# A transformer block on one Trainium2 core: a new order of the first transfers, with two large loads between and behind the stores of V

## The chip, the cores and the metric

One core of a Trainium2 chip. The metric is the device time of one launch in microseconds (us), lower is better. The kernel before has a median of 844.91 us over 3 runs (843.4 to 845.48).

## The reference

Two batch elements of 1024 positions with 128 features, all in float32:

```python
x = x + _layernorm(_L0_attn_ref(_layernorm(x), Wq, Wk, Wv, Wo, bo, rel_pos_bias))
x = x + _layernorm(_L0_ffn_ref(_layernorm(x), ...))      # one shared and 8 routed experts, top 2
# inside attention, 16 heads of 64:
q, k, v = x @ Wq, x @ Wk, x @ Wv                         # split into heads
logits = (q @ k.T + causal + pos_bias) / 64              # pos_bias: a table over 128 distances per head
out = (softmax(logits) @ v) @ Wo + bo
```

Each expert is a layer of 128 to 512 with GELU and one back to 128, weighted by a gate. The change touches only what lies ahead of the heads.

## The kernel before

The 2048 positions are 16 blocks of 128 (t = 0 to 15), in four quarters of four blocks. Products in float32 are made of three products of rounded halves: a tensor is split into a high part and the rest (`_hi`, `_lo`), and `three` (L1072) runs hi x hi, hi x lo and lo x hi.

**First stage, norm and V of all heads.** VectorE takes the quarters of x in turn (L815 to L827): statistics (L776, L779), a root on GpSimd (`root`, L418), Newton step and normalisation (L787 to L793). TensorE transposes each block (`transposes`, L1078), ScalarE and VectorE copy the result out as high and low part. Then `values_of_all(t)` (L1100) computes V of block t for all 16 heads, as two halves of 512 columns with three matmuls of 128x512 each, in four PSUM banks used in turn; so block t waits for the copies of block t - 2. ScalarE copies the first half and VectorE the second (`copy_v`, L613 and L808) into one of four SBUF buffers, `probs[t % 4]`, and SP stores the buffer, 512 KB, to DRAM (`store_v`, L311). A copy of block t waits until the store of block t - 4 has landed (`v_stored`). All four counts of stores are waited for (L351), then `load_v(0, 0)` brings back the columns of head 0 for the first batch element. GpSimd splits what is loaded (`split_v`, L451).

**Queues and hand-written order.** Every engine has a fixed program; nothing is planned at run time. All DMAs but two (the weight of V and bo, which ScalarE issues) are issued by SP, in program order, on one queue. SP's program is: the first loads, then for t = 0 to 15 the store of block t, with `place_q(0, 0)` (two DMAs, L320) behind t = 5 and `place_k(0, 0)` (L327) behind t = 7; then the waits for the stores, `load_v(0, 0)`, and `head(0)` (L333): `load_v(0, 1)`, `place_q(0, 1)`, `place_k(0, 1)`, and the same for the first batch element of the next head. `place_q` copies q between partitions once both halves are computed (`qk_lo`), `place_k` waits until q has been copied.

**Heads.** A head has 16 slots (s), one for each block of queries: scores on TensorE (`scores`, L1142; slot 8 is the first of the second batch element and waits for `k_copied`), row minimum with bias on VectorE (L848), exponential on ScalarE (L649), transposes of the probabilities (L1173), their product with V (L1191, first in slot 7), the output weight (L1205, first in slot 11). In slots 8 and 9 TensorE also computes q and k of the next head (`project_qk`), which waits for GpSimd's split of that head's weights (`split_wqk`, L423), in GpSimd's slot 5.

**Who reads what the change moves.** `wqk` is scaled by ScalarE at L627, behind two copies of transposed blocks and ahead of the first copies of V. `bias_all[:, 0]` is read by GpSimd at L521. `bias_all[:, 1:H]` is read by GpSimd in slot 0 of head 0 (L493), behind `split_v(0, 0)` in its program. `wo` is read by TensorE at L1205. `wr` and `layer_bias_T` (`small_loaded`) are read behind the last head (L567, L740, L981).

Of the kernel before, what the change touches and what calls it, by code (L numbers as in the profile page):

```python
# [11 lines left out]
def transformer_block(  # L12
# [23 lines left out]
    H = rel_steps.shape[1]  # L36
# [13 lines left out]
    NCH = NB // CH  # L50
# [48 lines left out]
    with ctx:  # L99
        def sb(name, shape, dt=f32):  # L100
            return ctx.enter_context(nc.sbuf_tensor(name, shape, dt))
# [4 lines left out]
        def sem(name):  # L106
            return ctx.enter_context(nc.semaphore(name))
# [11 lines left out]
        wo = sb("wo", [P, H, D])  # L119
        far = sb("far", [P, H])  # L120
        bias_all = sb("bias_all", [P, H, 2 * P])
# [32 lines left out]
        layer_bias_T = sb("layer_bias_T", [P, NE * HB + NE])  # L154
# [4 lines left out]
        wr = sb("wr", [P, E])  # L159
# [51 lines left out]
        wo_loaded = sem("wo_loaded")  # L211
        bo_loaded = sem("bo_loaded")
        acc_started = sem("acc_started")
        small_loaded = sem("small_loaded")
        bias_loaded = [sem(f"bias_loaded{i}") for i in range(2)]
# [75 lines left out]
        @block.sync  # L291
        def _(sp):
            def load_x(c):
                sp.dma_start(x_sb[:, CH * c:CH * (c + 1), :],
                             x_blocks[:, CH * c:CH * (c + 1), :]).then_inc(x_loaded[c], 16)

            load_x(0)
            load_x(1)
            sp.dma_start(wqk[:], Wqk).then_inc(wqk_loaded, 16)
            load_x(2)  # L300
            load_x(3)


            sp.dma_start(bias_all[:, 0:1, :], rel_steps[:, 0:1, :]).then_inc(bias_loaded[0], 16)
            sp.dma_start(bias_all[:, 1:H, :], rel_steps[:, 1:H, :]).then_inc(bias_loaded[1], 16)
            sp.dma_start(wo[:], Wo2).then_inc(wo_loaded, 16)
            sp.dma_start(wr[:], Wr).then_inc(small_loaded, 16)
            sp.dma_start(layer_bias_T[:], layer_bias).then_inc(small_loaded, 16)


            def store_v(t):  # L311
                sp.wait_ge(v_evac_act, t + 1)
                sp.wait_ge(v_evac_dve, t + 1)
                sp.dma_start(v_dram[t * P:(t + 1) * P, :], probs[t % 4][:]).then_inc(v_stored[t % 4], 16)

            def load_v(h, b):
                src = bass.AP(v_dram.tensor, h * DH + b * T * HD, [[HD, P], [P * HD, QB], [1, DH]])
                sp.dma_start(v_raw[b][:], src).then_inc(v_loaded[b], 16)

            def place_q(h, b):  # L320

                sp.wait_ge(qk_lo, h * (2 * B) + 2 * b + 2)
                for part in range(2):
                    sp.dma_start(q_hl[b][part * DH:(part + 1) * DH, :].bitcast(f32),
                                 k_hl[b][0:DH, part, :].bitcast(f32)).then_inc(q_copied[b], 16)

            def place_k(h, b):  # L327

                sp.wait_ge(q_copied[b], h * 32 + 32)
                sp.dma_start(k_hl[b][0:DH, :, :].bitcast(f32), k_hl[b][DH:P, :, :].bitcast(f32))\  # L330
                  .then_inc(k_copied[b], 16)

            def head(h, last=False):  # L333
                if not (isinstance(h, int) and h == 0):
                    sp.wait_ge(v_ready, h * B)
                load_v(h, 1)
                place_q(h, 1)
                place_k(h, 1)
                if not last:
                    sp.wait_ge(v_ready, h * B + 1)  # L340
                    load_v(h + 1, 0)
                    place_q(h + 1, 0)
                    place_k(h + 1, 0)

            for t in range(NB):
                store_v(t)
                if t == 5:
                    place_q(0, 0)
                if t == 7:
                    place_k(0, 0)  # L350
            for r in range(4):  # L351
                sp.wait_ge(v_stored[r], 16 * (NB // 4))
            load_v(0, 0)
            head(0)
            with sp.Fori(1, H - 1) as h:
                head(h)
            head(H - 1, last=True)

            def load_expert(i, wf, wp):
                sp.dma_start(wfc_raw[i], wf).then_inc(moe_w_loaded[i], 16)  # L360
                sp.dma_start(wproj_raw[i], wp).then_inc(moe_w_loaded[i], 16)


            sp.wait_ge(v_ready, (H - 1) * B + 1)
            sp.wait_ge(min_ready, (H - 1) * S + QB)
            load_expert(0, Wfc_s, Wproj_s.rearrange("(k p) n -> p k n", p=P))
            sp.wait_ge(v_ready, H * B)
            sp.wait_ge(min_ready, H * S)
            load_expert(1, Wfc[0, :, :], Wproj[0, :, :].rearrange("(k p) n -> p k n", p=P))

            def expert_src(e):

                return (bass.AP(Wfc.tensor, (e - 1) * (D * HID), [[HID, P], [1, HID]]),
                        bass.AP(Wproj.tensor, (e - 1) * (D * HID), [[D, P], [P * D, HB], [1, D]]))

            def reload(e, i):
                sp.wait_ge(wproj_ready, e - 1)
                load_expert(i, *expert_src(e))

            def load_gates(e, i):  # L380
                if not (isinstance(e, int) and e <= 2):
                    sp.wait_ge(gated_ready, (e - 1) * NCH)
                sp.dma_start(gate_rows[i], bass.AP(gate_dram.tensor, (e - 1) * (B * T), [[0, P], [1, B * T]]))\
                  .then_inc(gates_loaded[i], 16)

            reload(2, 0)
            sp.wait_ge(gate_T_ready, 1)
            for j in range(CH):
                sp.dma_start(bass.AP(gate_dram.tensor, j * P, [[B * T, E], [W, NCH], [1, P]]),
                             gate_T[j * E:(j + 1) * E, :, :]).then_inc(gates_stored, 16)  # L390
            sp.wait_ge(gates_stored, 16 * CH)
            load_gates(1, 1)
            load_gates(2, 0)
            with sp.Fori(3, NE - 1, 2) as e:
                for i in range(2):
                    reload(e + i, 1 - i)
                    load_gates(e + i, 1 - i)

            for c in range(NCH):
                sp.wait_ge(result_ready, c + 1)  # L400
                sp.dma_start(out_blocks[:, CH * c:CH * (c + 1), :],
                             normed[:, CH * c:CH * (c + 1), :]).then_inc(result_stored, 16)
            sp.wait_ge(result_stored, 16 * NCH)
# [667 lines left out]
        def _(pe):  # L1071
# [56 lines left out]
            def wait_shared(h, s, last):  # L1128

                uses = [u for u in SHARED_USE if u[0] < s and not (isinstance(h, int) and h == 0 and u[2] < 0)  # L1130
                        and not (last and u[2] > 0)]
                if isinstance(h, int) and h == 0 and not uses:
                    pe.wait_ge(qk_lo, NC)
                    return
                _, kind, n, b, part = uses[-1] if uses else SHARED_USE[-1]
                n = h + n if uses else h - 1
                if kind == "qk":
                    pe.wait_ge(qk_lo, n * (2 * B) + 2 * b + part + 1)
                else:
                    pe.wait_ge(wo_scaled, n * (B * NC) + b * NC + part + 1)  # L1140
# [249 lines left out]
```

## Time and profile before

| what | value |
|---|---|
| median of 3 runs | 844.91 us |
| the profiled execution | 844.46 us |
| its span | 842.7 us |
| TensorE matmuls (PE) | 771.5 us busy, 92% |
| VectorE (DVE) | 707.7 us, 84% |
| ScalarE (ACT) | 612.8 us, 73% |
| GpSimd (POOL) | 298.9 us, 35% |
| DMA | 70.72 MB, mean 84 GB/s |

Times in rows are in us from the start of the span unless marked ns. PE is TensorE's matmuls, PEld its weight loads, SPq and ACTq the issue of a DMA by SP or ScalarE. L12 is line 12 of the kernel. "x4" is the number of instructions merged into a row; in brackets stands how long the engine had been idle and what it waited for. The chain of waits is followed back from the last instruction: at each step to what released it. "issue" in it is time in which the engine waited for nothing that the profile shows. The granted clock is TensorE's, 1.00 for 2.4 GHz and 0.50 for 1.2 GHz.

### The profile page before, as it was taken

What the parts mean: (1) busy time and instruction counts of PE and PEld (TensorE: products, weight loads), DVE (VectorE), ACT (ScalarE), POOL (GpSimd) and SP (SyncE); (2) the same over time, 40 slices, a digit from 0 to 9 for tenths busy, and PEclk for the clock granted to TensorE, in tenths of its full rate; (3) what the DMA queues carried; (4) which work ended last, traced back from release to release, by engine and by line L of the source; (5) the groups of instructions that cost most, each with busy time, mean ns of one, the idle gap of its engine ahead of it and who ended that gap; (6) DMA issues with size and microseconds to landing.
All of it is one profiled execution on the core that took longest, in us unless ns stands there. A gap on an engine that the chain in (4) does not pass through costs nothing.

```text
span 842.7 us, 17198 instructions
## 1 busy us (share of the span) xinstructions
PE 771.5 (92%) x4436; PEld 657.1 (78%) x4436; DVE 707.7 (84%) x1596; ACT 612.8 (73%) x1340; POOL 298.9 (35%) x323
## 2 busy tenths in 40 slices
PE   3877999999999999999999999996489999999992
PEld 2656988888888888888889888885377777777771
DVE  5557888988888888888888888888778888898976
ACT  2356888887888888888788888873577767667672
POOL 2318823333332332333233233223503354445423
PEclk9899999999999999999999999999679999999997
DMA  7684334424423432442443343230003211122101
GB/s 279 219 280 89 75 66 97 88 62 87 100 62 76 95 77 62 93 94 62 87 95 67 70 97 82 62 75 26 25 1 129 76 60 43 46 75 75 51 1 50
DMA packets 56025, 70.72 MB, mean 84 GB/s; under 512 B 36032, under 2 KB 45120, under 8 KB 52544
## 3 DMA queue, kind: packets, MB, share of 16 engines
q1 hardware_dynamic: 55712, 69.83, 32.9%
q10 hardware_dynamic: 288, 0.59, 0.3%
q8 instruction: 11, 0.18, 0.1%
q14 instruction: 14, 0.11, 0.1%
HBM read 27.36 MB, written 9.50 MB: 44 GB/s over the span
## 4 chain that ended last, share of the span: by engine, by line
PE 75%; DVE 8%; issue 6%; POOL 4%; ACT 3%; DMA 3%; POOLq 0%; DVEq 0%; ACTq 0%; SPq 0%
PE out_ps L1191 16%; PE score_ps L1158 16%; PE trans_ps L1173 15%; PE shared_ps L1205 6%; PE trans_ps L1074 3%; PE score_ps L1074 3%; PE score_ps L1076 2%; PE score_ps L1075 2%; PE trans_ps L1075 2%; PE trans_ps L1076 2%; DVE pT_lo L961 2%; PE shared_ps L1074 2%; PE shared_ps L1076 2%; PE shared_ps L1075 2%; POOL rstd L421 1%
## 5 line engine op out<-in xcount | busy, mean ns | idle before, releaser
L649 ACT ACTIVATE probs<-score_ps,row_min 128x128 f32<-128x128 f32 (+7 forms) x256 | 189.9, 742 | 53.5 <-DVE row_min L848 53.4
L861 DVE TENSOR_TENSOR pT_lo<-trans_ps,pT_hi 128x512 fp32r<-128x512 f32 (+3 forms) x384 | 201.6, 552 | 16.7 <-ACT pT_hi L670 16.6
L670 ACT ACTIVATE pT_hi<-trans_ps 128x512 fp32r<-128x512 f32 (+3 forms) x384 | 185.1, 491 | 40.4 <-PE trans_ps L1173 28.8
L848 DVE CUSTOM_DVE_ANT_0 score_ps<-score_ps,bias 128x128 f32<-128x128 f32 (+7 forms) x256 | 194.6, 760 | 22.8 <-PE score_ps L1158 19.4
L1173 PE MATMUL trans_ps<-ident,probs 128*128 128x128 f32 x1152 | 190.0, 274 | 3.2 <-DVE pT_lo L861 1.8
L1158 PE MATMUL score_ps<-k_hl,q_hl 128*128 128x512 f32 (+2 forms) x768 | 182.5, 351 | 3.1 <-DMA k_hl<-k_hl 1.6
L470 POOL TENSOR_TENSOR acc<-acc,head_out 128x512 f32<-128x512 f32 x64 | 83.0, 1297 | 245.5 <-DVE head_out L879 245.3
L1173 PEld LDWEIGHTS trans_ps<-ident,probs 128*128 128x128 f32 x1152 | 136.8, 140 | 27.3 <-DVE pT_lo L861 11.9
L1191 PE MATMUL out_ps<-pT_hi,v_hl 128*128 128x512 f32 (+2 forms) x384 | 156.5, 409 | 1.1 <-DVE pT_lo L861 1.1
L961 DVE TENSOR_TENSOR pT_lo<-probs,pT_hi 128x512 fp32r<-128x512 f32 x144 | 133.2, 952 | 25.0 <-ACT pT_hi L728 15.1
L1158 PEld LDWEIGHTS score_ps<-k_hl,q_hl 128*128 128x128 f32 x768 | 134.4, 189 | 23.7 <-DMA k_hl<-k_hl 1.8
L735 ACT ACTIVATE probs<-score_ps,layer_bias_T 128x512 f32<-128x512 f32 x144 | 98.5, 686 | 56.1 <-PE score_ps L1076 52.1
L1191 PE MATMUL out_ps<-pT_lo,v_hl 128*128 128x512 f32 (+2 forms) x384 | 133.1, 347 | 0.0
L557 POOL TENSOR_TENSOR acc<-acc,head_out 128x512 f32<-128x512 f32 x32 | 44.0, 1375 | 112.7 <-DVE head_out L977 112.7
L1191 PEld LDWEIGHTS out_ps<-pT_hi,v_hl 128*128 128x128 f32 x384 | 72.7, 189 | 5.5 <-DVE pT_lo L861 1.3
L1191 PEld LDWEIGHTS out_ps<-pT_lo,v_hl 128*128 128x128 f32 x384 | 73.3, 191 | 4.3
L1205 PE MATMUL shared_ps<-wo,oT 128*128 (+1 forms) x512 | 70.0, 275 | 0.8 <-ACT oT L678 0.8
L805 DVE TENSOR_TENSOR k_hl<-shared_ps,k_hl 128x512 fp32r<-128x512 f32 x64 | 44.2, 691 | 30.0 <-ACT k_hl L611 30.0
L1205 PEld LDWEIGHTS shared_ps<-wo,oT 128*128 128x128 f32 x512 | 65.7, 191 | 3.5 <-issue 1.0
L728 ACT ACTIVATE pT_hi<-probs 128x512 fp32r<-128x512 f32 x108 | 68.0, 629 | 0.0
L1074 PE MATMUL trans_ps<-pT_hi 128*128 128x512 f32 x144 | 58.1, 403 | 5.1 <-DVE pT_lo L961 5.1
L1074 PE MATMUL score_ps<-nT_hi,pT_hi 128*128 128x512 f32 x144 | 57.6, 400 | 0.2 <-DVE nT_lo L799 0.2
(122 smaller groups left out, 1163.3 us busy)
## 6 DMA issues: line engine op xcount, KB each, us to landing
q_hl<-k_hl SPq DMA_DIRECT2D x64, 256.0 KB, 3.6
k_hl<-k_hl SPq DMA_DIRECT2D x32, 512.0 KB, 4.2
v_scratch<-probs SPq DMA_DIRECT2D x16, 512.0 KB, 4.0
v_raw<-v_scratch SPq DMA_DIRECT2D x32, 256.0 KB, 4.6
bias_all<-gate_scratch SPq DMA_DIRECT2D x8, 1024.0 KB, 4.8
v_raw<-in_Wfc SPq DMA_DIRECT2D x8, 256.0 KB, 4.9
bias<-in_Wproj SPq DMA_DIRECT2D x8, 256.0 KB, 5.3
bias_all<-in_rel_steps SPq DMA_DIRECT2D x1, 1920.0 KB, 12.7
```

The costliest lines, as they stand in the source:

```text
L470: pool.tensor_tensor(acc[:, blocks, :], acc[:, blocks, :], head_out[c][:].rearrange("p (t d) -> p t d", d=D), ALU.add)\
L649: act.activation(probs[s % 4][:, 0:n], scores_of(s % QB)[:, 0:n], ACT.Exp, bias=row_min[:, s:s + 1], scale=-1.0, accum_out=row_sum[:, s:s ...
L670: act.activation(pT_hi[c][:, CH * g:CH * g + m, q * P:(q + 1) * P], trans_ps[k % 2][:, 0:m * P].rearrange("p (m q) -> p m q", q=P), ACT.Co ...
L735: act.activation(hidden[c % 2][k], banks[k], ACT.Gelu_apprx_tanh, bias=layer_bias_T[:, bass.ds(e * HB + k, 1)]).then_inc(hidden_ready, 1)
L848: dve.tensor_tensor_reduce(out=ps, in0=ps, in1=bias_b[b][:, T - n:T], scale=1.0, scalar=3e38, op0=ALU.add, op1=ALU.min, accum_out=row_min[ ...
L861: dve.tensor_tensor(pT_lo[c][dst], trans_ps[k % 2][:, 0:m * P].rearrange("p (m q) -> p m q", q=P), pT_hi[c][dst], ALU.subtract).then_inc(p ...
L961: dve.tensor_tensor(lo, raw, hi, ALU.subtract).then_inc(hidden_lo_ready, 1)
L1074: pe.matmul(dst, w_hi, m_hi, start=start, stop=False)
L1158: last = pe.matmul(scores_of(i)[:, at:end], q, k_hl[b][:, part, at:end], start=part == 0, stop=part == 1)
L1173: last = pe.transpose(trans_ps[k % 2][:, o:o + P], probs[s % 4][:, j * P:(j + 1) * P], ident[:])
L1191: last = pe.matmul(out_ps[:, q0:W], v_hl[b][:, j, :], part[c][:, j, q0:W], start=j == 0 and part is pT_hi, stop=j == nk - 1 and part is pT_lo)
L1205: last = pe.matmul(shared_ps[:, j * P:(j + 1) * P], oT[c][:, j * P:(j + 1) * P], wo[:, h, :], start=True, stop=True)
```

## The change

SP's first issues are all four quarters of x, then the weight of q and k, then the bias of head 0. The bias of heads 1 to 15 is issued in the loop of the stores at t = 7, behind `place_k(0, 0)` and ahead of the store of block 8. The output weight, the router's weight and the layers' biases are issued behind `load_v(0, 0)` and ahead of `head(0)`. No other engine's program changes.

```diff
--- before.py
+++ after.py
@@ -294,18 +294,10 @@
                 sp.dma_start(x_sb[:, CH * c:CH * (c + 1), :],
                              x_blocks[:, CH * c:CH * (c + 1), :]).then_inc(x_loaded[c], 16)
 
-            load_x(0)
-            load_x(1)
+            for c in range(NCH):
+                load_x(c)
             sp.dma_start(wqk[:], Wqk).then_inc(wqk_loaded, 16)
-            load_x(2)
-            load_x(3)
-
-
             sp.dma_start(bias_all[:, 0:1, :], rel_steps[:, 0:1, :]).then_inc(bias_loaded[0], 16)
-            sp.dma_start(bias_all[:, 1:H, :], rel_steps[:, 1:H, :]).then_inc(bias_loaded[1], 16)
-            sp.dma_start(wo[:], Wo2).then_inc(wo_loaded, 16)
-            sp.dma_start(wr[:], Wr).then_inc(small_loaded, 16)
-            sp.dma_start(layer_bias_T[:], layer_bias).then_inc(small_loaded, 16)
 
 
             def store_v(t):
@@ -348,9 +340,13 @@
                     place_q(0, 0)
                 if t == 7:
                     place_k(0, 0)
+                    sp.dma_start(bias_all[:, 1:H, :], rel_steps[:, 1:H, :]).then_inc(bias_loaded[1], 16)
             for r in range(4):
                 sp.wait_ge(v_stored[r], 16 * (NB // 4))
             load_v(0, 0)
+            sp.dma_start(wo[:], Wo2).then_inc(wo_loaded, 16)
+            sp.dma_start(wr[:], Wr).then_inc(small_loaded, 16)
+            sp.dma_start(layer_bias_T[:], layer_bias).then_inc(small_loaded, 16)
             head(0)
             with sp.Fori(1, H - 1) as h:
                 head(h)
```

## Rows read from the trace of the kernel before

**Rows 1.** First line of the page.
```profile
span 842.7 us, 17198 instructions
```

**Rows 2.** Chain of waits in order of time: start, duration (us), what.
```profile
18.40 4.97 issue
...
29.07 0.43 PE score_ps L1074
...
41.24 6.14 DMA v_scratch<-probs
47.46 0.60 ACT probs L617
...
51.18 0.70 DVE probs L812
51.95 4.03 DMA v_scratch<-probs
...
59.36 0.62 POOL v_hl L456
```

**Rows 3.** Stretches: length, busy time (PE, PEld, DVE, ACT, POOL), clock, DMA share, GB/s.
```profile
25.00:30.00 5.00, 3.32 (x10) 2.84 (x11) 4.33 (x10) 1.19 (x2) 4.58 (x9) 0.59 0.26 104
30.00:35.00 5.00, 5.00 (x17) 3.92 (x17) 1.85 (x4) 1.79 (x3) 0.40 (x1) 0.72 0.53 211
...
40.00:45.00 5.00, 4.18 (x18) 2.80 (x16) 1.47 (x3) 0.85 (x2) 0.00 (x0) 1.00 1.02 323
45.00:50.00 5.00, 3.55 (x14) 2.63 (x15) 1.91 (x4) 1.62 (x4) 0.00 (x0) 1.00 1.00 408
...
65.00:70.00 5.00, 2.19 (x15) 1.58 (x13) 3.17 (x9) 3.43 (x8) 4.20 (x6) 1.00 0.49 105
```

**Rows 4.** Timeline of ScalarE: start, duration, instruction, [idle time before, releaser].
```profile
17.02 1.05 ACT L627 ACTIVATE wqk<-wqk 128x1024 f32<-128x1024 f32 x1
...
49.91 0.60 ACT L617 ACTIVATE probs<-score_ps 128x512 f32<-128x512 f32 x1 [0.63 <-DMA v_scratch<-probs]
```

**Rows 5.** Timeline of SP's DMA issues.
```profile
3.38 1.89 SPq L304 DMA_DIRECT2D bias_all<-in_rel_steps  x1
5.31 2.92 SPq L305 DMA_DIRECT2D bias_all<-in_rel_steps  x1
...
57.36 1.19 SPq L324 DMA_DIRECT2D q_hl<-k_hl  x2
62.85 0.46 SPq L330 DMA_DIRECT2D k_hl<-k_hl  x1
```

**Rows 6.** DMA issues, 0 to 80 us: KB each, median us to landing.
```profile
bias_all<-in_rel_steps SPq DMA_DIRECT2D x1, 1920.0 KB, 12.7
...
wqk<-in_Wqk SPq DMA_DIRECT2D x1, 1024.0 KB, 9.6
...
bias_all<-in_rel_steps SPq DMA_DIRECT2D x1, 128.0 KB, 10.1
```

**Rows 7.** Tile x_sb, 0 to 100 us: the time of its four loads.
```profile
DMA to landing us min/median/max: 4.8/8.7/10.3
```

**Rows 8.** Timeline of all engines: VectorE's statistics of the last quarter of x.
```profile
21.85 0.86 DVE L776 BATCH_NORM_STATS2 stats<-x_sb 128x6 f32<-128x128 f32 x4
```

**Rows 9.** Tile v_scratch, 0 to 80 us: the time of the 16 stores.
```profile
DMA to landing us min/median/max: 2.6/4.0/6.8
```

**Rows 10.** Timeline of TensorE: where it resumes after an idle time.
```profile
26.68 1.12 PE L1087 MATMUL trans_ps<-ident,normed 128*128 128x128 f32 x4 [2.92 <-DVE normed L793]
...
48.11 0.50 PE L1074 MATMUL score_ps<-pT_hi,nT_hi 128*128 128x512 f32 x1 [1.05 <-ACT probs L617]
...
67.12 0.51 PE L1158 MATMUL score_ps<-k_hl,q_hl 128*128 128x256 f32 x2 [1.55 <-DMA k_hl<-k_hl]
...
71.16 0.47 PE L1074 MATMUL shared_ps<-nT_hi,wqk_hl 128*128 128x512 f32 x1 [2.42 <-POOL wqk_hl L429]
```

**Rows 11.** Timeline of GpSimd: the second half of head 1's weight split.
```profile
70.56 0.46 POOL L429 TENSOR_TENSOR wqk_hl<-wqk,wqk_hl 128x128 fp32r<-128x128 f32 x1 [0.19 <-POOL wqk_hl L426]
```

## The prediction

> **What bounds the kernel now.** I read the page first for the scale [rows 1]: the profiled execution took 844.46 us, 1.76 us more than its span of 842.7 us, and the median of the three runs is 844.91 us. A measurement of this kernel can tell about 0.3%, 2.5 us, from no change. Every DMA that moves is issued in the first 60 us, so I then read the chain of waits there in order of time [rows 2]. The reader is to see that it goes through vector and tensor work until about 35 us, then through the DMA queue: the store of block 8 of V is issued at 41.24 and lands 6.14 us later, at 47.38. ScalarE's copy of block 12 into the same buffer starts at 47.46, the last store is issued at 51.95 and lands at 55.98, and GpSimd starts to split the V of head 0, loaded back behind it, at 59.36. The stretches [rows 3] say why a store takes so long: from 40 to 50 us the DMA engines are busy all the time (shares 1.02 and 1.00). This is the only part of the kernel so bound, and the change puts bytes into it.
>
> **Order of x and the first weight.** SP issues the same DMAs; the weight of q and k falls behind two quarters of x. Its issue ended before 3.38 [rows 5] and it landed 9.6 us after its issue [rows 6], so by 13.0 at the latest. Two quarters of x are 512 KB, as much as one store. ScalarE's copies, freed by stores that land one after another, start at 47.46 [rows 2] and 49.91 [rows 4] with one between: 1.225 us for 512 KB. So the weight lands by 14.2, while ScalarE scales it at 17.02 and does not wait for it [rows 4]. Cost 0; if the cover of 2.8 us were gone, a late weight would hold back ScalarE's copies of V. The last two quarters of x come earlier, but all four had landed at most 10.3 us after their issue [rows 7], with the last issue over by 3.38, so by 13.7. VectorE takes up the last quarter at 21.85, and no idle time stands before that row [rows 8]. Gain 0. The bias of head 0 keeps its place, behind the same bytes.
>
> **What leaves the start.** The bias of heads 1 to 15 (1920 KB), the output weight (1024 KB) and two small loads leave the queue between 5 and 21 us. Nothing in that stretch waits for a load but the two at its head (x and the weight of V), which stay ahead. The stores of V begin after it. Gain 0, at most what the front rival below gives.
>
> **The bias between the stores (term A).** It is now issued at t = 7, behind the copy of k and in front of the store of block 8. That store is what frees the buffer for block 12. The price of 1920 KB from two rows: 1920/512 x 1.225 = 4.6 us by the pace of the stores. In the first loads the bias of head 0 lands at 3.38 + 10.1 = 13.5 and the rest, the next in the queue, at 5.31 + 12.7 = 18.0, which is 4.5 us [rows 5, 6]. A bound from above is the rate of 323 GB/s from 40 to 45, where the copies between partitions run [rows 3]: 1.966 MB/323 GB/s = 6.1 us. I take 4.6, since these are long contiguous rows as in the first loads. The issue itself held SP for 2.92 us there [rows 5]; here that lies beside the transfer. Queued behind it on SP are the stores of 8 to 15, and behind these both halves of the load of V. ScalarE and VectorE wait with their copies of block 12, TensorE with block 14 for these copies. So copy 12 starts at 52.1. The bias has landed by then; GpSimd, its reader, is still busy with V's split after 59.36 + 4.6. **A = 4.6, bounds 4.5 and 6.1.**
>
> A rule beside this: the Trainium skill (DMA: Bandwidth & Descriptors, Anatomy of one DMA) fits one DMA of the GpSimd path as about 2 us plus the bytes at 436 GB/s. An estimate by that page would be 6.5 us for the bias and would make the sum 7.4 us. The two landings in a row, 4.5 us apart, speak against counting a fixed part in a full queue.
>
> **TensorE after the stall (term B).** TensorE's idle time ahead of block 14, at 48.11, is 1.05 us now; it grows by A to over 5.5. At 26.68 TensorE resumed after 2.92 us without work [rows 10], and the granted clock of 25 to 30 was 0.59 and of 30 to 35 was 0.72 [rows 3], a mixture of 1.2 and 2.4 GHz, with a matmul every 0.43 us [rows 2] instead of the (51.18 - 48.11)/12 = 0.26 of blocks 14 and 15 now. So I take blocks 14 and 15 at 1.2 GHz. Their 12 matmuls start 4.6 us after those of before, at 52.7, and take 12 x 0.43 = 5.2, until 57.9. VectorE's copy of the last half takes 0.7 (51.18 to 51.87 now), so the last store is issued at 58.7. It is then alone in the queue and lands after the shortest time seen, 2.6 us [rows 9], at 61.3. By A alone it would be 55.98 + 4.6 = 60.6. **B = 0.7, bounds 0 (full clock: the 3.1 us of matmuls are hidden by the stores) and 2.1** (5.2 - 3.1, all of it passed on).
>
> **The output weight behind the first load of V (term C).** V of head 0, half 0, is in front of it and pays nothing. Behind it on SP come three issues, each about as long as that of k (0.46 us) [rows 5], then V's other half, the two copies of q and the copy of k for the second batch element. 1024 KB are 2 x 1.225 = 2.45 us of queue. Now q is issued at 57.36, k at 62.85 [rows 5]; TensorE waits for k until 67.12, works until 71.16 - 2.42 = 68.74 and waits for GpSimd's split of the next head's weights [rows 10], which ends at 70.56 + 0.46 [rows 11]. So the path of k has 2.4 us to spare against GpSimd's. GpSimd moves by A + B = 5.3. The path of k moves with TensorE, whose head 0 starts after the copy that ends at 58.6 instead of 51.87, so by 6.7, and then by what is left of the output weight in the queue. That transfer runs from about 64.4 (V's half landed) to 66.9, V's other half until 68.2, while q is issued at 64.1; without it q would land at 69.6, with it at about 70.5, and k at 74.8. TensorE adds its 1.6 us: 76.4 against GpSimd's 71.16 + 5.3 = 76.5. That is a tie. **C = 0.2, bounds 0 and 2.5** (the whole transfer unhidden). The output weight is first read in slot 11, after 71.16; it lands by 67. The two small ones are read after the last head.
>
> **The sum.** 4.6 + 0.7 + 0.2 = 5.5 us on 844.46 gives 850.0 us, 5.1 us above the shown median. From 71.16 on TensorE follows itself in nearly every step, so nothing behind takes this back.
>
> **Rivals.**
> *Clock lost again in head 0.* The wait for k and the wait for GpSimd are now 1.55 and 2.42 us, with work between [rows 10], and the granted clock from 65 to 70 is 1.00 [rows 3]. In the new order they become one wait of some 2.5 us. If 1.2 GHz is granted after it as after the 2.92 us at 26.68, the loss is (1 - 0.59) x 5 + (1 - 0.72) x 5 = 3.4 us of TensorE's time [rows 3], where TensorE sets the pace: 853.4. The Trainium skill (TensorE: Matmul & The Clock Gate, Part 1) says that the slow level is the default and only activity lifts it, which would make this likelier. Against it: neither 1.55 nor 2.42 did it. Chance 0.2.
> *C in full.* If q and k also wait for the whole output weight, 852.3. Chance 0.08.
> *The stores slip past.* If stores and bias share the engines so that block 8 lands nearly as now and the tail needs less than all bytes, 1 to 2.5 us remain: 846.5. Against it: a queue busy at 1.00 until the last store was issued must still move 1920 KB more. Chance 0.07.
> *The front pays for it, and it is not slower.* The chain shows 4.97 us at 18.40 in which it names no releaser, ahead of the root of the last quarter [rows 2]. If that were a wait for x or for a start slowed by the large loads, the new order could take it away: 5.5 - 5.0 = 0.5, so 845.0, and below 844.9 if A is hidden by 0.6 us besides. It decides only if the last quarter of x lands after 21.85; the rows have it by 13.7 [rows 7, 8]. Chance 0.05.
>
> **How the numbers follow.** The forecast has 0.6. Its own range is from 849 (A at 4.5, B and C at 0) to 852.0. The last two rivals, 0.12 together, lie mostly below 847.5; of the clock rival about a third lies above 854. So 847.5 to 854.0 leaves out 0.2. Slower by over 0.3% means above 847.4: forecast, clock, C and the rest of the doubtful ones, 0.89. Within 0.3%: most of the two last rivals, 0.08. Faster 0.03.
>
> **What would show it.** In the profile after: the bias issued near 41 us; the longest store landing near 11 instead of 6.1 us; ScalarE's copy of block 12 at about 52 with a DMA wait of 6 to 7 us before it; granted clock below 1 between 50 and 60; GpSimd's split of V at about 64.5 instead of 59.36; TensorE's first weight projection of head 1 at 76.5 instead of 71.16; ScalarE's scaling still at 17.0 and VectorE's last quarter still at 21.9. The prediction is wrong if copy 12 comes before 50, or if the last quarter is taken up sooner than 21.

## The result, and the profile after

The changed kernel takes 855.48 us (median of 4 runs, 853.69 to 857.5) against 844.23 us for the kernel before (4 runs in all); the ratio is 1.0133 with a 95% interval of 1.0105 to 1.016. It is 11.25 us slower. The direction was forecast, the size was not: 5.5 us were, and 855.48 lies above the range. Two later sets of the same kernel gave 851.73 and 853.30 us (ratios 1.0093 and 1.0107); what differs between them is part of the answer below.

| | before | after |
|---|---|---|
| the profiled execution | 844.46 us | 855.13 us |
| its span | 842.7 us | 853.4 us |
| TensorE matmuls busy | 771.5 us | 776.2 us |
| VectorE, ScalarE, GpSimd busy | 707.7, 612.8, 298.9 us | 707.6, 613.9, 298.7 us |

The page after, its first line and the clock in 40 slices. The work of the engines is the same; the third and fourth slice (43 to 85 us) show a clock below full:

```profile
span 853.4 us, 17198 instructions
...
PEclk9978999999999999999999999999669999999996
```

SP's issues after. The weight of q and k goes out at 2.88; the bias of the later heads at 39.75, the eight stores behind it; the output weight at 62.41, ahead of q (64.71) and k (72.94). They answer to [rows 5]:

```profile
2.88 1.87 SPq L299 DMA_DIRECT2D wqk<-in_Wqk  x1
...
39.75 0.73 SPq L343 DMA_DIRECT2D bias_all<-in_rel_steps  x1
40.58 19.03 SPq L306 DMA_DIRECT2D v_scratch<-probs  x8
...
62.41 0.57 SPq L347 DMA_DIRECT2D wo<-in_Wo  x1
...
64.71 1.11 SPq L316 DMA_DIRECT2D q_hl<-k_hl  x2
72.94 0.46 SPq L322 DMA_DIRECT2D k_hl<-k_hl  x1
```

ScalarE's timeline after: the scaling of the weight, and the copies of blocks 11 and 12.

```profile
16.98 1.05 ACT L623 ACTIVATE wqk<-wqk 128x1024 f32<-128x1024 f32 x1
...
43.20 0.60 ACT L613 ACTIVATE probs<-score_ps 128x512 f32<-128x512 f32 x1 [2.04 <-DMA v_scratch<-probs]
52.52 0.60 ACT L613 ACTIVATE probs<-score_ps 128x512 f32<-128x512 f32 x1 [8.72 <-DMA v_scratch<-probs]
```

The scaling starts at 16.98 as against 17.02 [rows 4], so the later weight holds nobody. Copy 12 waits 8.72 us for a store. In the kernel before, copy 12 starts at 47.46 [rows 2] and copy 11 is this row:

```profile
44.74 0.60 ACT L617 ACTIVATE probs<-score_ps 128x512 f32<-128x512 f32 x1 [1.97 <-DMA v_scratch<-probs]
```

From copy 11 to copy 12 it was 2.72 us and is 9.32. This is the better measure of what the bias costs in the queue: **6.6 us**. In absolute time copy 12 moves by 5.06 only, because copy 11 came 1.54 us earlier, in an execution whose first slow stretch of TensorE (the granted clock of 25 to 30 is 0.74 here, 0.59 before [rows 3]) was shorter. Of the two later profiles of the same kernel, the second has no such head start (copy 11 at 44.65), the third has one of 1.3 us (43.40). The distance is steadier: in the nine executions profiled with all 1920 KB at this place it is 8.89 to 9.53 us, in the five with the bias at the start 2.66 to 2.78. So the bias costs 6.2 to 6.8 us here.

The chain of waits after, in order of time (start, duration, what), with the store of block 8, the last copy of V, the two copies for slot 8, and head 1's and head 2's first weight projection; then the same two projections in the kernel before:

```profile
40.58 11.86 DMA v_scratch<-probs
...
58.51 0.70 DVE probs L808
...
65.22 7.71 DMA q_hl<-k_hl
...
72.94 4.22 DMA k_hl<-k_hl
...
77.20 0.79 PE score_ps L1154 x2
...
80.13 0.43 PE shared_ps L1070
...
97.22 0.24 PE shared_ps L1070
```

```profile
71.16 0.47 PE shared_ps L1074
...
87.68 0.24 PE shared_ps L1074
```

The store of block 8 takes 11.86 us instead of 6.14 [rows 2]. Then a new piece stands in the chain: q takes 7.71 us, k 4.22, and TensorE resumes at 77.20 instead of 67.12. Head 1's projection starts 80.13 - 71.16 = 8.97 us later, head 2's 97.22 - 87.68 = 9.54. The span is 10.7 us longer, so 1.2 us more are lost behind this point. That is no more than executions differ by there: from head 2's projection to the end of the span it is 755.0 us before, 756.2 here and 754.4 in the second profile of the same kernel.

TensorE's waits after, and GpSimd's split of V and of head 1's weight:

```profile
53.17 0.79 PE L1070 MATMUL score_ps<-pT_hi,nT_hi 128*128 128x512 f32 x1 [7.66 <-ACT probs L613]
...
77.20 0.79 PE L1154 MATMUL score_ps<-k_hl,q_hl 128*128 128x256 f32 x2 [4.29 <-DMA k_hl<-k_hl]
```

```profile
65.03 0.61 POOL L452 CAST v_hl<-v_raw 128x512 fp32r<-128x512 f32 x1 [34.64 <-DMA v_raw<-v_scratch]
...
76.23 0.46 POOL L425 TENSOR_TENSOR wqk_hl<-wqk,wqk_hl 128x128 fp32r<-128x128 f32 x1 [0.19 <-POOL wqk_hl L422]
```

Before block 14 TensorE waits 7.66 us instead of 1.05, before slot 8 4.29 instead of 1.55 [rows 10], and there is no wait for GpSimd behind it: its split ends at 76.69, before TensorE even resumes. In the stretches of 5 us (length, busy time of PE, PEld, DVE, ACT, POOL, granted clock, DMA share, GB/s):

```profile
45.00:50.00 5.00, 0.51 (x3) 0.08 (x1) 0.00 (x0) 0.00 (x0) 0.00 (x0) 0.79 0.99 327
50.00:55.00 5.00, 1.83 (x4) 1.49 (x5) 1.38 (x2) 1.20 (x2) 0.00 (x0) 0.50 1.00 410
55.00:60.00 5.00, 4.01 (x12) 2.84 (x11) 1.38 (x2) 1.20 (x2) 0.00 (x0) 0.69 0.74 302
...
75.00:80.00 5.00, 2.79 (x12) 2.70 (x13) 0.84 (x3) 0.60 (x1) 4.15 (x8) 0.52 0.49 105
```

From 45 to 50 the engines move only 327 GB/s at a share of 0.99, where the stores moved 408 in the same stretch before [rows 3]; at 327 GB/s the 1.966 MB of the bias take 6.0 us. The clock is at 1.2 GHz all through 50 to 55, behind the first wait, and again at 75 to 80 (0.52), behind the second.

So the 8.97 us at head 1's projection come apart: 76.69 - 71.02 = 5.67 is V's delay, as GpSimd passes it on. TensorE's resume at 77.20 and its usual 1.62 us of work (71.16 - 2.42 - 67.12 [rows 10]) would end at 78.82, 2.0 us behind GpSimd's time for it (71.16 + 5.67). The work takes 2.93 instead of 1.62 us at the slow clock: 1.3. The sum is 5.67 + 2.0 + 1.3.

### The profile page after: what moved, and what is told of

Same layout as the page of the kernel before. It is cut to its first block, busy times and chain, and to the rows that moved or that the text cites. A ratio compares the mean times of both kernels' runs of the same rounds, so it can differ in the third digit from the quotient of the medians.

```text
span 853.4 us, 17198 instructions
## 1 busy us (share of the span) xinstructions
PE 776.2 (91%) x4436; PEld 660.3 (77%) x4436; DVE 707.6 (83%) x1596; ACT 613.9 (72%) x1340; POOL 298.7 (35%) x323
## 4 chain that ended last, share of the span: by engine, by line
PE 73%; DVE 8%; issue 6%; DMA 5%; ACT 3%; POOL 3%; DVEq 0%; ACTq 0%; POOLq 0%; SPq 0%
PE out_ps L1187 16%; PE score_ps L1154 15%; PE trans_ps L1169 15%; PE shared_ps L1201 6%; PE score_ps L1070 3%; PE score_ps L1071 3%; PE trans_ps L1070 3%; PE score_ps L1072 3%; DVE pT_lo L957 2%; PE trans_ps L1071 2%; PE trans_ps L1072 2%; PE shared_ps L1070 2%; DMA v_scratch<-probs 2%; PE shared_ps L1071 2%; PE shared_ps L1072 2%
## 5 line engine op out<-in xcount | busy, mean ns | idle before, releaser
L1187 PEld LDWEIGHTS out_ps<-pT_hi,v_hl 128*128 128x128 f32 x384 | 72.9, 190 | 5.5 <-DVE pT_lo L857 1.3
L452 POOL CAST v_hl<-v_raw 128x512 fp32r<-128x512 f32 x32 | 19.6, 612 | 111.8 <-PE out_ps L1187 76.9
```

What stands on the lines that cost most here:

```text
L1187: last = pe.matmul(out_ps[:, q0:W], v_hl[b][:, j, :], part[c][:, j, q0:W], start=j == 0 and part is pT_hi, stop=j == nk - 1 and part is pT_lo)
```

## The experiments

Two theories stood after this. **Theory:** the bias costs its place in the queue of stores, the output weight delays the copy of k beyond what GpSimd hides, and TensorE's clock falls behind both waits. **Rival:** the output weight is hidden, as the prediction had it, and all comes from the bias and what follows its stall. The ratios are to runs of the kernel before on the same chip, with their 95% intervals.

**The front alone.** Against the kernel before:

```diff
-            load_x(0)
-            load_x(1)
+            for c in range(NCH):
+                load_x(c)
             sp.dma_start(wqk[:], Wqk).then_inc(wqk_loaded, 16)
-            load_x(2)
-            load_x(3)
```

> Only the order of x and the weight of q and k is changed, the two large loads stay at the start. Both theories put the whole loss elsewhere: within 0.3% of the kernel before (842 to 847 us), ScalarE's scaling of the weight still near 17.0 us and VectorE's last quarter still near 21.9. If the new order at the front had a part in the loss or hid a gain, it would show here as more than 2.5 us.

843.87 us against 843.8, ratio 0.9996 (0.9986 to 1.0007). The order at the front is worth nothing, neither way. The rival of a front that pays for the rest is gone.

**The bias alone.** The first loads keep their order, only the bias of heads 1 to 15 moves behind `place_k(0, 0)`:

```diff
-            sp.dma_start(bias_all[:, 1:H, :], rel_steps[:, 1:H, :]).then_inc(bias_loaded[1], 16)
...
                     place_k(0, 0)
+                    sp.dma_start(bias_all[:, 1:H, :], rel_steps[:, 1:H, :]).then_inc(bias_loaded[1], 16)
```

> Only the bias of heads 1 to 15 moves between the stores; the output weight stays at the start. Theory (queue, then a second wait behind the output weight): the bias costs its time in the queue, 5 to 5.9 us, with 0.7 more for blocks 14 and 15 at the slow clock, and TensorE then still waits for GpSimd and not for k: 850 us. Rival (all comes from the bias, through the stall and the slow clock behind it): nearly the whole loss of 11 us stays, 854 to 856 us.

852.09 us, ratio 1.0097 (1.0083 to 1.0112): 8.2 us, between what the two theories gave. ScalarE's copies of blocks 11 and 12, then TensorE's waits, then head 2's first projection in the chain:

```profile
41.60 0.60 ACT L617 ACTIVATE probs<-score_ps 128x512 f32<-128x512 f32 x1 [2.02 <-DMA v_scratch<-probs]
50.61 0.60 ACT L617 ACTIVATE probs<-score_ps 128x512 f32<-128x512 f32 x1 [8.41 <-DMA v_scratch<-probs]
```

```profile
51.26 0.80 PE L1074 MATMUL score_ps<-pT_hi,nT_hi 128*128 128x512 f32 x1 [7.37 <-ACT probs L617]
...
71.16 0.50 PE L1158 MATMUL score_ps<-k_hl,q_hl 128*128 128x256 f32 x2 [0.32 <-DMA k_hl<-k_hl]
...
75.16 0.47 PE L1074 MATMUL shared_ps<-nT_hi,wqk_hl 128*128 128x512 f32 x1 [2.18 <-POOL wqk_hl L429]
```

```profile
93.16 0.23 PE shared_ps L1074
```

The copies stand 9.01 us apart, 6.3 more than before. But in slot 8 TensorE waits 0.32 us for k and 2.18 for GpSimd, much as before [rows 10]: without the output weight, k is not late. This execution, the fastest of its four with 850.25 us, had a granted clock of 1.00 from 25 to 30 and so a head start of 3.1 us at copy 11. Head 1's projection is 4.0 us later than before, head 2's 5.5: between them the clock of 75 to 80 is 0.66, behind the wait for GpSimd, where it was 1.00 before from 70 to 80.

**The output weight and the small loads alone.** The kernel before with these three behind the first load of V:

```diff
             load_v(0, 0)
+            sp.dma_start(wo[:], Wo2).then_inc(wo_loaded, 16)
+            sp.dma_start(wr[:], Wr).then_inc(small_loaded, 16)
+            sp.dma_start(layer_bias_T[:], layer_bias).then_inc(small_loaded, 16)
             head(0)
```

> Only the output weight and the two small loads move behind the first load of V. Theory: the copy of k lands some 4.4 us later than its 67.1 us, of which GpSimd's wait hides 2.4, so 2 us, and up to 2.4 us more if TensorE is granted the slow clock after the long wait: 846 to 849 us. Rival (the output weight is hidden behind GpSimd, as the prediction's term C had it): within 0.3%, 844 to 845 us.

847.73 us, ratio 1.0035 (1.0022 to 1.0049), 3.0 us by the ratio. TensorE's wait in slot 8, the stretch around it, and head 2's first projection in the chain:

```profile
71.75 0.79 PE L1158 MATMUL score_ps<-k_hl,q_hl 128*128 128x256 f32 x2 [6.17 <-DMA k_hl<-k_hl]
```

```profile
70.00:75.00 5.00, 3.25 (x13) 3.06 (x14) 1.05 (x3) 0.89 (x2) 4.25 (x7) 0.53 0.38 82
```

```profile
92.05 0.23 PE shared_ps L1074
```

k is 4.6 us later than the 67.12 of before, the wait is 6.17 us, and the clock is 0.53 behind it. The rival falls: these loads are not hidden. The three moved together, 1024 KB and 26.5 KB in small ones; no run takes them apart. The parts add up to 0 + 8.2 + 3.0 = 11.2 us. That is the loss of the first set, but the later two lost 7.9 and 9.0 us by their ratios, so the sum does not show that the parts are independent.

**The output weight behind k.** The changed kernel, with the three loads issued behind `place_k(0, 1)` in `head(0)`:

```diff
-            sp.dma_start(wo[:], Wo2).then_inc(wo_loaded, 16)
...
                 place_k(h, 1)
+                if isinstance(h, int) and h == 0:
+                    sp.dma_start(wo[:], Wo2).then_inc(wo_loaded, 16)
...
```

> The changed kernel with the output weight and the small loads issued behind the copy of k of head 0 instead of ahead of it. Theory: the wait for k falls back to where GpSimd hides it and the second stretch at the slow clock goes: about 850 us, 4 to 6 us less than the changed kernel. Rival (bias alone): no change against the changed kernel, 854 to 856 us.

851.16 us, ratio 1.0095 (1.008 to 1.011). The time is that of the bias alone, and so are the waits of TensorE in slot 8. By time alone the gain over the changed kernel is not shown: it is 3 us against the first set (1.0133), 1 us against the third (1.0107) and none against the second (1.0093), and the changed kernel did not run in this one.

```profile
72.60 0.50 PE L1155 MATMUL score_ps<-k_hl,q_hl 128*128 128x256 f32 x2 [0.47 <-DMA k_hl<-k_hl]
...
76.36 0.47 PE L1071 MATMUL shared_ps<-nT_hi,wqk_hl 128*128 128x512 f32 x1 [2.10 <-POOL wqk_hl L426]
```

**Half of the bias.** The changed kernel with heads 1 to 8 loaded at the start:

```diff
+            sp.dma_start(bias_all[:, 1:9, :], rel_steps[:, 1:9, :]).then_inc(bias_loaded[1], 16)
...
-                    sp.dma_start(bias_all[:, 1:H, :], rel_steps[:, 1:H, :]).then_inc(bias_loaded[1], 16)
+                    sp.dma_start(bias_all[:, 9:H, :], rel_steps[:, 9:H, :]).then_inc(bias_loaded[1], 16)
```

> The changed kernel with the bias of heads 1 to 8 left at the start and that of heads 9 to 15 (896 KB) between the stores. Theory (the bias costs its time in the queue and a share of slow clock behind the wait): the store of block 8 lands 2.6 us later than if nothing were ahead of it instead of 5.6, so 3 us less than the changed kernel, 851.5 to 853 us. Rival (a fixed cost of a load between stores, such as a turn of the queue from stores to loads): less than 1 us is gained, 854 to 856 us.

850.64 us, ratio 1.0082 (1.0069 to 1.0095), 0.9 us below what was expected. The copies of blocks 11 and 12:

```profile
41.50 0.60 ACT L614 ACTIVATE probs<-score_ps 128x512 f32<-128x512 f32 x1 [1.95 <-DMA v_scratch<-probs]
47.69 0.60 ACT L614 ACTIVATE probs<-score_ps 128x512 f32<-128x512 f32 x1 [5.59 <-DMA v_scratch<-probs]
```

They are 6.19 us apart, so 896 KB cost 3.5 us. With the 6.3 us of 1920 KB in the bias-only run, whose copy 11 stands at the same place (41.60), this gives 2.8/1024 KB, or 2.75 us for 1000 KB, and 1.0 us that does not go with the bytes. The pace of the stores is 2.4 us for 1000 KB. So the rival in its strong form falls, since most of the price goes with the bytes, but a part of it holds; both numbers rest on one execution each. The issue of these 896 KB also held SP for 2.64 us, that of the 1920 KB for 0.75, so the bytes are not all that differs between the two points.

**Matmuls in the waits.** The changed kernel with matmuls that nobody reads, 28 ahead of TensorE's wait for copy 12 and 16 ahead of its wait for k:

```diff
+                    if t == 14 and half == 0:
+                        for _ in range(28):
+                            pe.matmul(out_ps[:], wv_hi[:, 0:P], nT_hi[:, 0:W], start=True, stop=True)
...
+                if isinstance(h, int) and h == 0 and s == QB:
+                    pe.wait_ge(qk_lo, 2 * B)
+                    for _ in range(16):
+                        pe.matmul(shared_ps[:], v_hl[0][:, 0, :], nT_hi[:, 0:W], start=True, stop=True)
```

> The changed kernel with 28 matmuls of 128x512 that nobody reads in TensorE's wait ahead of block 14 and 16 more in its wait for the copy of k in slot 8. They lie in waits of 7.7 and 4.3 us and add nothing to the result. Theory (part of the loss is the clock of 1.2 GHz granted after these waits): the clock stays at 2.4 GHz up to 90 us, blocks 14 and 15 take 3 us instead of 5.3, head 1 starts at full speed, 3 us less than the changed kernel: 851.5 to 853 us. Rival (the clock hides behind the DMAs): 854 to 856 us.

851.18 us, ratio 1.009 (1.0065 to 1.0116). With the first group alone:

> Only the 28 matmuls ahead of block 14. Theory: the blocks 14 and 15 come at full speed and are then held by the stores, so 0.5 to 1 us are won there, and the clock still falls in the wait for k: 854 to 855 us, at least 1 us more than with both fillers. Rival (the first slow stretch is the one that costs): same time as with both.

853.84 us, ratio 1.0117 (1.0102 to 1.0131). This looked like the theory. But the two intervals overlap, and the changed kernel itself had not been run beside them; the next set shows why that matters.

**The changed kernel again, and both parts with filled waits.**

> The changed kernel again, beside the others on this chip, as a measure for them: 853.5 to 857.5 us, a ratio of 1.011 to 1.016.

851.73 us, ratio 1.0093 (1.0079 to 1.0107), less than expected. Here is an execution of the same code 3.6 us shorter than the first one (851.50 against 855.13). ScalarE's copies of blocks 11 and 12, GpSimd's split, TensorE's resume in slot 8, the first projections of heads 1 and 2 in the chain, and two stretches:

```profile
44.65 0.60 ACT L613 ACTIVATE probs<-score_ps 128x512 f32<-128x512 f32 x1 [1.98 <-DMA v_scratch<-probs]
53.85 0.60 ACT L613 ACTIVATE probs<-score_ps 128x512 f32<-128x512 f32 x1 [8.60 <-DMA v_scratch<-probs]
```

```profile
78.07 0.46 POOL L425 TENSOR_TENSOR wqk_hl<-wqk,wqk_hl 128x128 fp32r<-128x128 f32 x1 [0.19 <-POOL wqk_hl L422]
```

```profile
77.37 0.51 PE L1154 MATMUL score_ps<-k_hl,q_hl 128*128 128x256 f32 x2 [1.95 <-DMA k_hl<-k_hl]
```

```profile
79.00 0.23 PE shared_ps L1070
...
95.30 0.23 PE shared_ps L1070
```

```profile
65.00:70.00 5.00, 5.00 (x18) 4.21 (x17) 3.46 (x10) 3.13 (x9) 2.78 (x5) 0.50 1.10 336
...
75.00:80.00 5.00, 3.05 (x21) 2.54 (x20) 2.89 (x9) 3.41 (x9) 4.14 (x8) 1.00 0.51 108
```

There is no head start (copy 11 at 44.65, copy 12 at 53.85, so 6.4 us later than before), V is late by 7.5 us, and TensorE resumes for k 0.17 us later than in the first profile. Why that is not more, though V's load, the output weight and q are issued 1.5 to 2.2 us later, is not shown. But the slow clock falls into 65 to 70, where TensorE waits for k afterwards anyway, and 75 to 80 is at 1.00. The wait for k is 1.95 us and head 1 starts at full speed. Head 1's projection is late by 7.84 us, of which 7.51 are V's delay (GpSimd's split ends at 78.53 instead of 71.02): in this execution the output weight costs next to nothing. Head 2's projection comes 1.9 us earlier than in the first profile; the other 1.8 of the 3.7 us between the two spans lie behind it, and no row here explains them. So where a slow stretch falls against the two waits decides over some 2 us, with the same code.

The bias alone, with 28 matmuls ahead of block 14 and 8 ahead of head 1's first projection (the same lines as above at those places):

> Only the bias moved, with 28 matmuls that nobody reads ahead of block 14 and 8 ahead of head 1's first weight projection in slot 8, where TensorE waits 2.2 us for GpSimd. Theory (queue time 5.2 to 5.7 us, the rest of this part's 8.2 is the clock): 849 to 850.5 us. Rival (the clock costs nothing, the stores' delay passes on with something else): 851.5 to 853 us as without them.

850.06 us, ratio 1.0069 (1.0056 to 1.0082), as the theory had it and below the 1.0083 to 1.0112 without them. The output weight alone, with 26 matmuls in the wait for k:

> Only the output weight and small loads moved, with 26 matmuls that nobody reads in the wait for the copy of k in slot 8 (6.2 us). Theory: the copy of k comes 4.6 us later, GpSimd's wait hides 2.4 of it, so 2.2 us stay and the clock's part of 1 to 2 us goes: 845.5 to 846.5 us. Rival: 847.5 us as without them.

845.58 us, ratio 1.0012 (1.0002 to 1.0022) instead of 1.0035 (1.0022 to 1.0049). In the parts, which were not run beside their unfilled copies, some 2 us each go. Head 2's first projection in the chain, for the bias and for the output weight:

```profile
90.79 0.23 PE shared_ps L1074
```

```profile
89.48 0.24 PE shared_ps L1074
```

The profiles say the same without the medians. With the bias, TensorE starts block 14 at 51.24 with the fillers and 51.26 without, and head 2's projection at 90.79 instead of 93.16; the clock of 75 to 80 is 1.00 instead of 0.66. With the output weight it resumes for k at 71.56 and 71.75, and head 2's projection comes at 89.48 instead of 92.05; the clock of 70 to 75 is 1.00 instead of 0.53. From head 1's projection to head 2's it is 16.53 us with the bias filled, 16.52 before and 18.00 unfilled, so of the 2.4 us won there 1.5 lie behind the wait for GpSimd and 0.9 ahead of it, in blocks 14 and 15. From the resume for k to head 2's projection it is 17.92 and 20.30, so 2.4 us lie behind the wait for k. All this is one execution each.

**Side by side.** Both versions of the whole change in the same rounds:

> The changed kernel once more, beside its filled copy. Both theories: 851 to 857 us. Where the second slow stretch falls is what sets the place in that range: if it begins behind TensorE's wait for the copy of k it costs some 2 us more than if it begins ahead of that wait.

> The changed kernel with 28 + 16 matmuls that nobody reads in the two waits. Theory (the clock is a part of the loss): 2 to 4 us less than the changed kernel beside it, 850 to 851.5 us, about the sum of the two parts with filled waits (5.8 + 1.0 us over the kernel before). Rival (the clock hides behind the DMAs): the same time as the changed kernel beside it, within 1 us.

853.30 us (1.0107, 1.0086 to 1.0127) and 853.16 us (1.0117, 1.0094 to 1.014). The medians do not differ; here the expected gain was missed. The profile of the filled kernel shows the clock held through both waits:

```profile
50.00:55.00 5.00, 3.81 (x16) 2.55 (x14) 2.07 (x3) 1.79 (x3) 0.00 (x0) 1.00 1.03 419
...
75.00:80.00 5.00, 4.66 (x32) 4.29 (x33) 3.15 (x9) 3.40 (x8) 4.43 (x6) 1.00 0.21 47
```

Yet its six runs are 850.2, 850.6 and 851.8 us with a mean granted clock of 0.976 to 0.978, and 854.6, 855.7 and 855.9 with 0.972 to 0.973. In half of the runs the clock was lower all the same, and those are 3 to 6 us longer; no profile shows where it fell. In the twelve filled runs of both sets the seven at 0.976 or more took 847.8 to 852.1 us, the five at 0.974 or less 852.6 to 856.0. So within the filled kernel the time goes with the clock, run by run. Across versions it does not: the unfilled runs of the second set have 0.965 to 0.969 and took 851.2 to 853.3. That the fillers win anything in the median of the whole change is not shown. The twelve filled runs have a median of 851.9, the fifteen unfilled ones of all sets 853.3.

**Both loads where nothing is behind them.** The changed kernel with the bias behind the store of block 1 and the output weight behind k:

```diff
                 store_v(t)
+                if t == 1:
+                    sp.dma_start(bias_all[:, 1:H, :], rel_steps[:, 1:H, :]).then_inc(bias_loaded[1], 16)
...
                 place_k(h, 1)
+                if isinstance(h, int) and h == 0:
+                    sp.dma_start(wo[:], Wo2).then_inc(wo_loaded, 16)
...
```

> The changed kernel with the same two loads moved to where nothing is behind them: the bias behind the store of block 1 (the DMA engines idle from about 25.5 to 29 us), the output weight behind the copy of k of head 0. Theory: the loss is only where the bytes stand in the queue and what the waits do to the clock, so all of it goes: within 0.3% of the kernel before, 843 to 846 us. Rival (leaving the start costs something by itself): 847 us or more.

843.75 us, ratio 1.0002 (0.9991 to 1.0012). SP's issues, and the stretch that takes the bias up:

```profile
22.34 0.68 SPq L344 DMA_DIRECT2D bias_all<-in_rel_steps  x1
...
61.62 0.59 SPq L332 DMA_DIRECT2D wo<-in_Wo  x1
```

```profile
25.00:30.00 5.00, 3.38 (x17) 2.87 (x18) 4.96 (x11) 1.80 (x3) 4.58 (x10) 1.00 1.00 377
```

The DMA share of 25 to 30 is 1.00, where it was 0.26 before [rows 3]. The same bytes, issued 17 us earlier, cost nothing. Leaving the start is free; the places were what cost.

**GpSimd's work in its idle time.** The wait of 2.42 us for GpSimd, which had hidden part of the output weight, can itself go. The kernel before, with its order of loads, shapes the biases ahead of the wait for V:

```diff
             take_bias(0, 0)
+            pool.wait_ge(bias_loaded[1], 16)
+            then_wait(pool.tensor_copy(far[:, 1:H], bias_all[:, 1:H, 0]))
+            for h in range(1, H):
+                shape_bias(h)
+            pool.wait_ge(bo_loaded, 16)
+            for b in range(B):
+                pool.tensor_copy(acc[:, QB * b:QB * (b + 1), :],
+                                 bo_all[:].unsqueeze(1).broadcast_to([P, QB, D])).then_inc(acc_started, 1)
             split_v(0, 0)
```

The same steps leave GpSimd's slots of head 0.

> The kernel before, with its order of loads, but GpSimd shapes the biases of heads 1 to 15 and copies bo in its idle time from 30 to 59 us, ahead of its wait for V, which needs the bias at the start. If TensorE's wait of 2.4 us in slot 8 is GpSimd's chain of these steps, it goes: 841 to 842.5 us against 844. If the work on GpSimd ends after V has landed, or slows the copies of the other engines, the gain is gone or reversed: 844 to 848.

840.79 us against 843.91, ratio 0.9958 (0.9945 to 0.9971): faster than both kernels. GpSimd's timeline:

```profile
56.17 2.02 POOL L520 COPY acc<-bo_all 128x1024 f32<-128x1024 f32 x2
58.15 0.61 POOL L456 CAST v_hl<-v_raw 128x512 fp32r<-128x512 f32 x1
...
60.90 0.46 POOL L429 TENSOR_TENSOR wqk_hl<-wqk,wqk_hl 128x128 fp32r<-128x128 f32 x1 [0.18 <-POOL wqk_hl L426]
```

The last preparation runs up to 58.15, where the split of V starts, and head 1's weight is split by 61.4 instead of 71.0. The first preparation of a later head's bias starts at 30.23, so this needs the bias by then; the change issues it at 39.75 only.

## Why the prediction was right in direction and wrong in size

**The front: right.** Cost and gain 0 were forecast and 0.07 us measured. ScalarE's scaling stayed at 17.0.

**Term A, mis-sized.** 4.6 us were taken, with bounds of 4.5 and 6.1; the copies of blocks 11 and 12 move apart by 6.2 to 6.8, which is above even the bound. Copy 12 waits 8.72 us for its store, where 6 to 7 were forecast. The step that failed is "I take 4.6, since these are long contiguous rows as in the first loads". The difference of two landings in the first loads has no place for what a load costs beside its bytes at a change of kind, and the two points above give 1.0 us for that, with a rate that is also below the pace of the stores. The copy of k ahead of the bias lands 6.3 us after its issue instead of 5.5, so a part of it may lie there. The Trainium skill (DMA: Bandwidth & Descriptors, Anatomy of one DMA), whose fit of about 2 us plus the bytes at 436 GB/s gave 6.5 us and which I set aside, comes near the whole, but it is a fit of the GpSimd path, and SP issues this load. Its parts do not agree: an estimate by it is 4.1 us for 896 KB, where 3.5 were measured, and the two points give 1.0 us beside the bytes and 372 GB/s. Why the rate is lower here than that of the stores stays open.

**Term B: right.** Blocks 14 and 15 ran at 1.2 GHz. The last copy on VectorE ends at 59.2, where 58.6 was forecast; V is split at 65.03, where about 64.5 was. The longest store took 11.86 us, where 11 was. That these two held in absolute time owes 1.5 us to the head start; without it, in the second profile, the copies come 6.4 and V 7.5 us late.

**Term C, mis-sized by its neighbour.** 0.2 us were taken, from a tie between 76.4 for TensorE and 76.5 for GpSimd. GpSimd came as forecast (76.69). TensorE came at 78.82 by its waits and 80.13 by its clock, so 3.3 us of the 8.97 lie beyond V's delay. The step that failed is the landing of q, "with it at about 70.5": it was 65.22 + 7.71 = 72.9. The output weight, V's other half and both copies of q took longer than the pace of the stores that I gave them, and k starts only when q is there. Alone, the move costs 3.0 us. Here the loss depends on a difference of two paths of 76 us, and a tie was no reason for a term of nearly nothing. In the second profile the tie did come true (78.53 for GpSimd, 79.00 for TensorE, a term of 0.3 us). There the error is in A, 6.4 us where 4.6 were taken, and with 1.1 for B head 1 is late by 7.8 us and the end of the span by 7.0, against the forecast 5.5. The medians of the two later sets lie inside the range, so a part of the first miss is the spread between sets of one program.

**The rival "clock lost again in head 0": it came true,** in the first and the third profile of the changed kernel (0.52 and 0.50 at 75 to 80 us), at 0.2 chance, and in the weight-only run; not in the second profile (1.00). It was put as an alternative to "C in full", while the second is what makes the wait long enough for the first: 4.29 us, where 2.5 had been worked out. The length of the wait alone does not decide, though: the clock fell behind 2.18 us in the bias-only run and not behind 2.42 in the kernel before. Both together on the forecast give 850.0 + 2.3 + 3.4 = 855.7. That this meets the measured 855.48 is luck, since term A stands in it with 4.6 us. Separate chances for linked cases made the range too narrow at its top.

**"From 71.16 on TensorE follows itself, so nothing behind takes this back": right,** but it loses 0.6 us more in head 1, and 1.2 behind that, which is within what executions differ by there. The rival in which the stores slip past the bias falls with the copies of block 12.

## What to carry to other kernels

Before a load is moved, look at what stands behind it at the new place: the kernel lost 8 us by 1920 KB put in front of stores that free buffers, and nothing by the same bytes 17 us earlier in a gap. Where two paths meet within a microsecond, price the later one with the rates of its own kind of transfer, and treat the long wait and the slow clock behind it as one case. Compare versions of a kernel with such waits only side by side.

## What the runs showed of the hardware

The same 1920 KB cost 6.2 to 6.8 us between stores and copies, and landed 4.5 us behind the load ahead of them in the first loads. One program had medians of 851.7, 853.3 and 855.5 us in three sets, and runs from 849.9 to 857.5, while the kernel before stays between 842.6 and 845.7 in all of them. In one execution the slow stretch (0.50 from 65 to 70) fell ahead of a wait and was hidden by it, in another (0.52 from 75 to 80) behind it, where 1.62 us of work took 2.93. In the pairs with and without matmuls in the waits, the slow clock cost 1.5 us behind a wait of 2.2 us and 2.4 us behind one of 6.2, up to head 2's projection.
